# Third expert layer in token halves, 24 of its results fetched inside its loop, bias rows ahead of its gathers, second weights' halves side by side

## What is computed

```python
probs = softmax(layernorm(x) @ Wr.T)                # 8 experts
p, e = top_k(probs, 2); p = p / sum(p)
out = sum(p[k] * (gelu(layernorm(x) @ W1[e[k]] + b1[e[k]]) @ W2[e[k]] + b2[e[k]]) for k in (0, 1))   # 128 -> 512 -> 128
```

## Time and profile before

| | us |
|---|---|
| median of 3 runs (lowest, highest) | 1114.45 (1113.37, 1115.78) |
| the profiled execution's own time | 1116.47 |
| its span in the trace | 1114.7 |

### The profile page before, as it was taken

The page is one execution under the profiler, slowest core; times in us unless marked ns, Lnnn a source line. Parts: engine busy times, 40 slices in busy tenths (PEclk is TensorE's granted clock), DMA queues, the critical chain, the costliest instruction groups (busy, mean ns, idle before and its releaser), DMA issues.

```text
span 1114.7 us, 20298 instructions
## 1 busy us (share of the span) xinstructions
PE 674.6 (61%) x5992; PEld 531.0 (48%) x5992; DVE 723.4 (65%) x2283; ACT 524.2 (47%) x1160; POOL 540.8 (49%) x562
## 2 busy tenths in 40 slices
PE   7115853589810586343899981488872569977900
PEld 7013531277710354343688870255552458766700
DVE  7884675989988355677355663599988636533542
ACT  3611333756550133251577871377762258755700
POOL 0007656586100562642676766465112656574475
PEclk9998985789955599555799995699885679988965
DMA  9602321000020133121233331111000123222242
GB/s 300 171 0 48 91 60 48 19 4 2 2 76 0 42 83 70 47 81 28 59 85 77 82 62 50 31 36 36 25 29 29 38 58 83 66 69 63 55 109 71
DMA packets 82502, 66.40 MB, mean 60 GB/s; under 512 B 10665, under 2 KB 74026, under 8 KB 82402
## 3 DMA queue, kind: packets, MB, share of 16 engines
q1 hardware_dynamic: 68674, 37.09, 11.5%
q0 software_dynamic: 13728, 28.02, 11.4%
HBM read 38.99 MB, written 26.08 MB: 58 GB/s over the span
## 4 chain that ended last, share of the span: by engine, by line
PE 24%; DVE 15%; issue 8%; another core or an unknown queue 6%; POOL 6%; ACT 3%; DMA 2%; DVEq 1%; POOLq 0%; ACTq 0%
POOL rt L1284 5%; PE bank L741 4%; PE bank L759 3%; PE bank L743 3%; PE bank L762 3%; PE bank L742 3%; PE bank L760 2%; DVE turned L1114 2%; PE bank L725 1%; DVE x L1172 1%; POOL ytok_loop L1284 1%; DVE arena L2025 1%; DMA rt<-y_moe,slot_i 1%; DVE arena L2018 1%
## 5 line engine op out<-in xcount | busy, mean ns | idle before, releaser
L1261 POOL DMA_INDIRECT turned<-xrows_moe,token x234 | 252.0, 1077 | 326.6 <-DVE token L1034 203.2
L1284 POOL DMA_INDIRECT rt<-y_moe,slot_i x176 | 174.9, 994 | 140.1 <-DVE x L1172 54.6
L817 ACT ACTIVATE turned<-bank,b1T 128x256 f32<-128x256 f32 (+1 forms) x372 | 131.5, 445 | 104.2 <-PE bank L743 47.1
L741 PE MATMUL bank<-rt,w1h 128*128 128x128 bf16 (+1 forms) x528 | 139.2, 264 | 27.9 <-issue 9.7
L759 PE MATMUL bank<-w2h,turned 128*128 x780 | 147.8, 224 | 10.0 <-issue 4.9
L760 PE MATMUL bank<-w2h,turned 128*128 x780 | 147.4, 224 | 9.8 <-issue 9.7
L1114 DVE TENSOR_TENSOR turned<-turned 128x1024 bf16<-128x1024 f32 (+1 forms) x119 | 127.3, 1070 | 34.0 <-ACT turned L822 19.0
L762 PE MATMUL bank<-w2l,turned 128*128 x780 | 133.8, 224 | 11.5 <-issue 10.9
L742 PE MATMUL bank<-rt,w1h 128*128 128x128 bf16 (+1 forms) x528 | 137.3, 261 | 1.7 <-issue 1.6
L743 PE MATMUL bank<-rt,w1l 128*128 128x128 bf16 (+1 forms) x528 | 137.0, 260 | 1.2 <-issue 1.2
L808 ACT ACTIVATE turned<-bank 128x512 f32<-128x512 f32 x40 | 24.0, 599 | 165.9 <-issue 86.4
(11 more groups left out here) (331 smaller groups left out, 1666.3 us busy)
## 6 DMA issues: line engine op xcount, KB each, us to landing
y_moe<-arena SPq DMA_DIRECT2D x119, 128.0 KB
xrows_moe<-xn SPq DMA_DIRECT2D x8, 512.0 KB
turned<-xrows_moe,token POOLq DMA_INDIRECT x234
rt<-y_moe,slot_i POOLq DMA_INDIRECT x176
x<-in_x SPq DMA_DIRECT2D x4, 512.0 KB, 5.9
arena<-in_w SPq DMA_DIRECT2D x1, 2048.0 KB, 9.6
xn<-in_w SPq DMA_DIRECT2D x8, 256.0 KB, 4.8
xrows_moe<-arena SPq DMA_DIRECT2D x4, 512.0 KB
```

The costliest lines, as they stand in the source:

```text
L741: nc.tensor.matmul(o, wh, xh_t, start=True, stop=False)
L817: last = nc.scalar.activation(s["h32"][:, t % 2, o:o + width], bank[1 + 2 * (t % 2) + u // 2][:, at:at + width], ACT.Gelu, bias=b1T[:, ds( ...
L1261: nc.gpsimd.indirect_dma_start(out=s["xs"][:, 2 * (t % BODY) + j], out_offset=None, in_=s["xdram"], in_offset=bass.IndirectOffsetOnAxis(ap ...
L1284: nc.gpsimd.indirect_dma_start(out=brought_to(s, n), out_offset=None, in_=s["ydram"][0:P * UNITS] if s["halves"] == 2 and at < PART else s ...
```

## The change

Four things are done.
1. The third layer gets the last layer's form: `halves=2`, slots aligned to 128, 40 rows (24 pure, 16 mixed) in place of 39 pure ones, `ahead=8`.
2. It fetches 24 of its 64 results inside its loop, 3 behind each of the rows 32 to 39 (`first_steps`); they are those of the unit's first three steps. DVE combines them inside the loop too, and `combine` and `gau_rows_pool` skip them (`landed`). ACT waits before the unit's first heads until the third layer's rows are stored.
3. `gau_rows` goes ahead of the third layer's gathers, without its wait for them.
4. The second weights lie side by side, [128, expert, chunk, high and low, 128]. A chunk and tile of `down` is then one matmul of 256 columns (high hidden values by high and low weights, into neighbouring columns `y` and `ylow` of the bank) and one of 128 (low hidden values by high weights). `finish` adds `ylow`: where there is a bias by one more DVE operation of 128 x 256 behind the bias addition (L1148 of the changed kernel), in the first two layers by a reduction over the two parts in place of the copy.

The core of the diff:

```diff
-        PAIRS = dict(moe0=UNITS // 2, moe2=UNITS // 2, moe3=-(-(2 * T // W + E - 1)), moe6=UNITS)
+        PAIRS = dict(moe0=UNITS // 2, moe2=UNITS // 2, moe3=UNITS, moe6=UNITS)
...
-            s["align"] = W if stage == "moe3" else P
-            s["pure"] = [stage == "moe3" or halves == 2 and t % (UNITS // 2) < PURE for t in range(n // 2)]
+            s["landed"] = {n for ns in s["amid"].values() for n in ns}
+            s["pure"] = [halves == 2 and t % (UNITS // 2) < PURE for t in range(n // 2)]
...
-            PER = 1 if s["align"] == W else 2
+            PER = 2
...
-                y = [bank[5 + r][:, P * j:P * j + P] for j in range(2)]
-                w2hf, w2lf = (w[:].rearrange("p e c n -> p (e c) n") for w in (w2h, w2l))
+                both = [bank[5 + r][:, W * j:W * j + W] for j in range(2)]
+                y = [bank[5 + r][:, W * j:W * j + P] for j in range(2)]
+                w2f = w2[:].rearrange("p e c i n -> p (e c i n)").rearrange("p (a i) -> p a i", i=2)
...
-                    for group in (js,) if s["pure"][t] else [(j,) for j in js]:
-                        wh, wl = (w[:, ds(e[group[0]] + P * u, P)] for w in (w2hf, w2lf))
-                        for j in group:
-                            nc.tensor.matmul(y[j], hh[j], wh, start=(u + j == 0), stop=False)
-                            nc.tensor.matmul(y[j], hl[j], wh, start=False, stop=False)
-                        for j in group:
-                            last = nc.tensor.matmul(y[j], hh[j], wl, start=False, stop=(u == FC - 1 and j == js[-1]))
+                    for j in js:
+                        first = e[0] if s["pure"][t] else e[j]
+                        w = w2f[:, ds(first + P * u, P)].rearrange("p a i -> p (a i)")
+                        nc.tensor.matmul(both[j], hh[j], w, start=(u + j == 0), stop=False)
+                        last = nc.tensor.matmul(y[j], hl[j], w[:, 0:P], start=False, stop=(u == FC - 1 and j == js[-1]))
...
+                    dve.wait_ge(*s.at("biased", t + 1))
+                    js = tiles_of(s["stage"], t)
+                    nc.vector.tensor_tensor(ysb[:, k % YRING, 0:js], ysb[:, k % YRING, 0:js], ylow[:, 0:js], ALU.add)\
+                        .then_inc(s["y"], 1)
                 else:
-                    nc.vector.tensor_copy(ysb[:, k % YRING], y).then_inc(s["y"], 1)
+                    js = tiles_of(s["stage"], t)
+                    nc.vector.tensor_reduce(ysb[:, k % YRING, 0:js], bank[5 + k % 2][:, 0:W * js].rearrange("p (j i n) -> p j n i", i=2, n=P),
+                                            AX, ALU.add).then_inc(s["y"], 1)
...
+                if n in s["landed"]:
+                    continue
                 combine_one(dve, s, n)
...
             pool.wait_ge(au["rb"], 3)
-            for k in range(BODY):
-                pool.wait_ge(gathered[k], GATHERED[k][moe3["index"] + 1])
...
+                if j == 0:
+                    results_stored(act, moe3, moe3["pairs"])
...
+        first_steps = {t: [3 * (t - AMID), 3 * (t - AMID) + 1, 3 * (t - AMID) + 2] for t in range(AMID, UNITS)}
...
-        moe3 = moe("moe3", ln3, 2, **W1, order=by_steps, back=2 * QUAD)
+        moe3 = moe("moe3", ln3, 2, **W1, order=by_steps, halves=2, ahead=BODY, back=2 * QUAD, amid=first_steps)
...
             ln_rows_pool(pool, ln3)
-            moe_pool(pool, moe3, gau_rows)
+            gau_rows(pool)
+            moe_pool(pool, moe3)
             gau_rows_pool(pool, moe3)
```

More of the change, by code:

```diff
@@ L191, in program @@
         per_e = sb("per_e", [P, 10, 2 * E])
-        assert UNITS % BODY == 0 and UNITS >= PAIRS["moe3"]
+        assert UNITS % BODY == 0
         starts = sb("starts", [1, 3, 2 * UNITS])
@@ L243, in program @@
         splits = []
-        for st, hi, lo, loads in ((st_w1_1, w1h1, w1l1, ("w1", 16)), (st_w2_1, w2h1, w2l1, ("w1b", 16 * E))):
-            spec = "p a b -> p (a b)" if st is st_w1_1 else "p a b c -> p (a b c)"
-            splits.append((st, hi[:].rearrange(spec), lo[:].rearrange(spec), loads))
+        for st, hi, lo, loads in ((st_w1_1, w1h1, w1l1, ("w1", 16)), (st_w2_1, w2_1[:, :, :, 0], w2_1[:, :, :, 1], ("w1b", 16 * E))):
+            if st is st_w1_1:
+                part = lambda a, o: a.rearrange("p e f -> p (e f)")[:, o]
+            else:
+                part = lambda a, o: a.rearrange("p e c n -> p (e c) n")[:, o.start // P:o.stop // P]
+            splits.append((st, hi, lo, part, loads))
         PIECES = E * F1 // SPLIT
@@ L258, in cast, with like @@
                     o = slice(E // 2 * (i - 6), E // 2 * (i - 5))
-                    nc.scalar.activation(w2h0[:, o], st_w2_0[:, o], ACT.Copy).then_inc(pr["w0h"], 1)
+                    nc.scalar.activation(w2_0[:, o, :, 0], st_w2_0[:, o], ACT.Copy).then_inc(pr["w0h"], 1)
             return cast
+        def like(a, b):
+            return a if len(b.shape) == len(a.shape) else a.rearrange("p (c n) -> p c n", n=P)
         def split_high(act):
-            for st, hi, lo, (q, v) in splits:
+            for st, hi, lo, part, (q, v) in splits:
                 act.wait_ge(ld[q], v)
@@ L267, in split_high @@
                     o = slice(SPLIT * i, SPLIT * (i + 1))
-                    nc.scalar.activation(hi[:, o], st[:, o], ACT.Copy).then_inc(pr["w1h"], 1)
+                    h = part(hi, o)
+                    nc.scalar.activation(h, like(st[:, o], h), ACT.Copy).then_inc(pr["w1h"], 1)
         def split_low(dve, which):
-            st, hi, lo, loads = splits[which]
+            st, hi, lo, part, loads = splits[which]
             for i in range(PIECES):
@@ L275, in split_low @@
                 dve.wait_ge(pr["w1h"], PIECES * which + i + 1)
-                nc.vector.tensor_tensor(lo[:, o], st[:, o], hi[:, o], ALU.subtract).then_inc(pr["w1l"], 1)
+                h = part(hi, o)
+                nc.vector.tensor_tensor(part(lo, o), like(st[:, o], h), h, ALU.subtract).then_inc(pr["w1l"], 1)
         def rows_pool(pool):
@@ L477, in logits @@
                 for t in range(TPS * i, TPS * (i + 1)):
-                    last = nc.tensor.matmul(bank[6][:, E * t:E * t + E], xnT[:, P * t:P * t + P], router,
+                    at = E * place(of, t)
+                    last = nc.tensor.matmul(bank[6][:, at:at + E], xnT[:, P * t:P * t + P], router,
                                             start=True, stop=True)
@@ L579, in tiles_of @@
         def tiles_of(stage, t):
-            return 1 if stage != "moe3" and t % (UNITS // 2) == UNITS // 2 - 1 else 2
+            return 1 if t % (UNITS // 2) == UNITS // 2 - 1 else 2
         def gathered_by(s, t):
@@ L622, in moe @@
                                        xhi=(2 - K) * (n // 2), onehot=2 * K,
-                                       inv=2 * K, idx=halves, half=(K - 1) * NT, turned=n // 2, up=n // 2, gelu=n // 2 * bias, comb=NT,
+                                       inv=2 * K, idx=halves, half=(K - 1) * NT, turned=n // 2, up=n // 2, gelu=n // 2 * bias, biased=n // 2 * bias, comb=NT,
                                        **{q: RINGS[q] + n // 2 for q in RINGS}))
@@ L825, in moe_scalar @@
                 act.wait_ge(ld["consts2"], 64)
-                per = 1 if s["align"] == W else 2
+                per = 2
                 for t in range(s["pairs"]):
@@ L1057, in moe_vector @@
             sums = [rt[0:1, 5, units * i:units * (i + 1)] for i in range(2)]
[L1058 removed]
+            first_slot = starts[:, 2, 0:units]
             if H == 1:
@@ L1121, in finish @@
                 dve.wait_ge(ystored[k % YRING], YSTORED[k % YRING][s["index"]] + 16 * turns)
-                y = bank[5 + k % 2][:, 0:W].rearrange("p (j n) -> p j n", j=2)
+                y, ylow = (bank[5 + k % 2][:].rearrange("p (j i n) -> p j i n", j=2, i=2)[:, :, i] for i in range(2))
                 if s["bias"]:
-                    unit = 2 * t if A == P else t
+                    unit = 2 * t
                     if unit % BODY == 0:
@@ L1280, in bring_one @@
             t, k, nth = result(s, n)
+            back = ring if n in s["landed"] else back
             if n >= back:
@@ L1739, in gau_rows_pool @@
                 for n in range(2 * QUAD * j, 2 * QUAD * (j + 1)):
-                    bring_one(pool, s, n)
+                    if n not in s["landed"]:
+                        bring_one(pool, s, n)
                 if j >= 7:
```

32 lines of the change are left out of this document (16 added, 16 removed).

## The result

| | before | after |
|---|---|---|
| median of 5 runs (lowest, highest), us | 1113.6 (1113.15, 1115.78) | 1121.95 (1120.05, 1123.88) |
| profiled execution, us | 1116.47 | 1120.05 |
| PE instructions | 5992 | 5392 |
| DVE busy, us | 723.4 | 771.1 |

The change is slower: ratio 1.0071, interval 1.0052 to 1.009. The forecast was 1107.5 and faster; the time lies inside the range, on the side to which I gave 0.33.

What follows compares the result with a forecast made beforehand. POOL's indirect DMAs, PE idling beside them and mixed rows' matmul groups bound the kernel. Terms −3 +9 +1 +26 +2 −26 −13 −3 sum to −7 from 1116.5: 1109.5 profiled, median 1107.5 us, range 1088 to 1128.

Steps and rivals of the forecast that it cites:

- Results in the crowded rows: Third loop's rows that also fetch results: 24 results take 6.25 us of POOL a row, +26 us.
- start: Third loop's first five rows: slow as in the last layer, partly relieved by fewer PE matmuls, +9 us.
- mixed and pure rows: Third layer: mixed rows cost +6.1 us, less 3.6 by fewer matmuls and 1.5 in pure rows, together +1 us.
- last layer and tail: Last layer: mixed rows, start, crowded and pure rows gain by PE's shorter program, −13 us; tail 0.
- first layers: First two layers: `down` takes 8 matmuls for 12, against a longer DVE reduction, −3 us.
- loop's end to the first heads: Between third loop and first heads: the wait for stores and two steps' results go, −26 us.
- End of the loop: Third loop's last rows: +8.5 us as in the last layer, less 3.6 and 2.8, together +2 us.
- Routing: Third routing to first gather: halves give −5.3 us, bias rows slowing DVE cost +2.3, together −3 us.
- the first: Third loop's start and crowded rows: POOL sets the pace, PE's shorter program relieves nothing; 1127 us, chance 0.27.
- The second: All rows: the number of PE's matmuls and weight loads holds them, 8 of 40 fewer shorten each; 1088 us, chance 0.16.
- The third: Third loop: results merely move, start +13 and crowded rows +30 us, last layer −13; 1115.5 us, chance 0.14.

Runs made afterwards that it cites:

- g1: Change with 16 results inside the third loop and the bias rows behind row 14's gathers; 1132.85 us, ratio 1.017 to the kernel before (1114.82 us).
- e9: The same kernel as g1, in another run; 1141.43 us, ratio 1.0159 to the kernel before (1122.39 us).
- g2: Change with no results inside the third loop; 1117.54 us, ratio 1.0022 to the kernel before (1114.82 us).
- g3: Second weights side by side alone, third layer and bias rows as in the kernel before; 1098.39 us, ratio 0.9833 to the kernel before (1114.82 us).
- e1: The same kernel as g3, in another run; 1008.14 us, ratio 0.9965 to the kernel before (1012.96 us).
- e5: Change with 16 results inside the third loop in place of 24; 1008.66 us, ratio 0.9943 to the kernel before (1013.63 us).
- f2: The same kernel as e5, in another run; 1006.57 us, ratio 0.9922 to the kernel before (1015.35 us).
- c1: The change itself, run again; 1017.22 us, ratio 1.0034 to the kernel before (1013.63 us).

## Why the prediction was wrong

Right: the two big terms and the sign of nearly each. Results in the crowded rows +20.3 (forecast +26, bounds 20 to 32), start +11.0 (+9; 5 to 13), mixed and pure rows −0.1 (+1; −2 to +5), last layer and tail −8.2 (−13; −4 to −20), first layers −5.2 (−3; −6 to +3), loop's end to the first heads −27.5 (−26; −28 to −22). A sum of −7 with terms of 26 on either side turns on little. Some of this is luck. The first gather came the foretold 3 us earlier (3.6), but from the first layers' −5.2 and routing's +1.6. The start was taken down from 12.9 because a fifth of the crawl would go; the last layer's own start, the same rows with the same gathers, only went from 46.9 to 44.5.

Two steps failed, and alone they turn the sign (+10.6 and +4.6 on −7):
1. *End of the loop.* "+8.5 in the last layer; −3.6 …; −2.8 … Together +2", bounds −1 and +8; it is +12.6. I took the last layer's end as the model, where sixteen results are through before it. With three results a row POOL has five issues in place of four, and the last of 24 are issued beside the loop's last rows: the end to its last low part takes 38.6 us with 24, 30.9 and 30.4 with sixteen (g1, e9) and 29.4 with none (g2). The price of the eight more results, "5 × 1.25 = 6.25 a row", I put on the crowded rows alone, and there it does not show: they take 46.5 us with 24, 46.4 and 47.0 with sixteen. I didn't look up that the ring holds 16 results (the changed kernel has it: `back = ring if n in s["landed"] else back`); what the wait for it costs by itself is not shown.
2. *Routing.* "over 14 us of which DVE would be slowed in part I take +2.3"; it is +6.4, beyond my bound's 5.5 for DVE, while the halves gave 4.8 of the 5.3, so the term is +1.6 and not −3 (still inside its bounds of −5.3 and +3). The bound scaled DVE's times by 2.01/1.22, as if a long instruction paid in proportion. What is paid is a wait per instruction. The rule that I quoted from the Trainium skill, "SBUF — State Buffer", § Who interferes with whom, speaks of DVE instructions with two SBUF inputs, and by it I leaned to −5. L1006 and L1013 are TENSOR_SCALARs; the same section says that such ones can enter a mode that takes both ports, and that whoever issues first, DVE or GpSimd, then holds the pair for its whole instruction while the other is blocked. The rows agree with that sentence (1.04 for 0.17 us, 2.15 for 0.24), and I had left it out; in which mode L1006 and L1013 ran, no trace shows.

The sum misses the profiled execution by 10.6 us (1120.05 for 1109.5). The other 3.9 us to the median are the spread of the runs: I took the median 2.0 below the profiled execution, as before, and it lies 1.9 above. The last layer, −8.2 for −13, is the next largest miss: PE's shorter program gives little where POOL issues (first rows −2.4, crowded rows −1.8).

Of the rivals, the first had the right sign and the right resource on the first kind of chip, but the wrong place: POOL sets the pace not in rows 22 to 29 (22.8 us with results or without) but behind them. Its price of 1127 is nearer to 1121.95 than mine. Its clause that PE's shorter program relieves nothing nearly holds where it was meant: in g3 the last layer's first rows gain 1.6 us and its crowded rows 2.5; the rest of g3's gain lies elsewhere. The second's pace of 2.9 us a pure row does exist, on the first kind of chip, but with the old weights as well. The third, results that merely move, is nearest to what g2 shows: 31.6 for 25.9. What holds PE up beside POOL stays open: I had read it as instructions that come late.

The split on the second kind, from traces and ratios: weights −18.6 us (g3), halves with the start eight ahead and the bias rows first +21 (g2 against g3, 0.0189 of 1114; of it 11.9 in the first five rows, 4.9 in rows 12 to 19, 1.7 in routing and 5.7 in the end with its one row more), results +5.5 (the change against g2): together +8. The three were measured on more than one chip, each against the kernel before there.

The best kernel: e1/g3, the weights alone, beats both on both kinds (0.9833; 0.9965 and 0.9931). Sixteen results inside (e5, f2) are as good or better on the first kind (0.9943 and 0.9922) and were not run on the second.

## What to carry to other kernels

When work is moved into a loop on an engine's queue, price its whole length there, not the rows at which it is written: a lead of eight rows only says where the bill comes, and moving eight transfers behind the last one that the loop needs gave 8 us back (on the first kind of chip). Look up the ring that a moved transfer writes into, and count how many fit. Two sums of 26 us against each other are no forecast of their difference; changes that come bundled should be run part by part, since here, on the second kind, one part was worth −1.7% and the rest took it all back.

## What was new of the hardware

The same kernel takes 1013 us on some chips and 1114 to 1122 on others. By the traces of one kernel on both (e1 and g3, 90 us apart) 39 us of it lie in the last loop, 16 in the third and 30 ahead of the third routing, where the first layers' loops are. The largest single steps are where POOL issues indirect DMAs without a pause: rows 22 to 29 with 24 results between the gathers take 22.8 us (c1) and 46.5 us (the change's first trace), the last layer's first five rows 30.2 and 44.5. POOL's own issues are 1.25 us apart on both. But calm rows differ too: a pure row takes 2.9 us on the one kind and 3.2 to 3.3 on the other. Where POOL issues, PE's time goes into gaps without a recorded wait; the granted clock is lower there as well (0.74 for 1.00 in rows 22 to 29), behind the idle time. I don't know the cause; no run here looked at PE's instruction supply by itself. And the bias rows' effect on DVE, on both kinds: two instructions that take 0.24 us together take 2.15 when POOL operations of 1 to 2.4 us run beside them, and the same operation reading PSUM does not pay.
